# A decoder's second layer: the attention sink added by the tensor engine, the cosine product left in PSUM, and a small subtraction moved to GpSimd

## The reference, cut to what matters

```
x = x + _L1_attn_ref(layernorm(x), ...)          # "D" below
x = x + _L1_xattn_ref(layernorm(x), ctx, ctx, ...) # "E": attention of each row's 16 heads among themselves
x = x + _L1_ffn_ref(layernorm(x), ...)           # "F": causal attention that gates a two-branch product, then "M"
...
att = einsum('bhqd,bhkd->bhqk', q, k) * hd ** (-0.5) + sink      # D, hd = 16, one sink value per head
att = softmax(att);  out = einsum('bhqk,bhkd->bqhd', att, v)
...
mod = 0.1 * tanh(attn @ A)                                        # F
gate = silu(h @ W_in.T + mod * (h @ A) @ B);  up = h @ W_up.T     # M
out = residual + (gate * up) @ W_down.T
```

## Time and profile before

| what | value |
|---|---|
| time, median of 3 runs | 3060.1 us (3059.43 to 3067.85) |
| the profiled execution, its own time | 3064.77 us, of which the span 3063.0 us |
| busy share of the span | PE 90%, PEld 75%, DVE 84%, ACT 64%, POOL 69% |
| granted PE clock, mean over the span | 0.951 |
| largest groups of layer two | POOL L1802 380.4 us, POOL L1795 358.6 us, DVE L2324 151.7 us |

### The profile page before, as it was taken

The page is one execution under the profiler, slowest core; times in us unless marked ns, Lnnn a source line. Parts: engine busy times, 40 slices in busy tenths (PEclk is TensorE's granted clock), DMA queues, the critical chain, the costliest instruction groups (busy, mean ns, idle before and its releaser), DMA issues. The chain is left out here.

```text
span 3063.0 us, 68267 instructions
## 1 busy us (share of the span) xinstructions
PE 2760.3 (90%) x22128; PEld 2307.7 (75%) x22128; DVE 2565.5 (84%) x5547; ACT 1954.2 (64%) x4120; POOL 2126.1 (69%) x2651
## 2 busy tenths in 40 slices
PE   6999999999999999999788499558899999999978
PEld 3888888888888888888455399436777777777767
DVE  6888888888888888888499577488999999999973
ACT  5888778788787878878344155345656565565642
POOL 5897666666666666666378455288888888888870
PEclk9999999999999999999899699768999999999999
DMA  4564344444344444443444599300000000000000
GB/s 144 172 206 161 130 151 130 149 133 150 128 130 145 142 138 142 147 138 112 139 152 145 190 334 336 132 14 19 17 27 19 27 19 25 21 24 22 20 5 11
DMA packets 186021, 340.09 MB, mean 111 GB/s; under 512 B 40810, under 2 KB 104179, under 8 KB 179075
## 3 DMA queue, kind: packets, MB, share of 16 engines
q1 hardware_dynamic: 179586, 319.55, 31.8%
q0 software_dynamic: 6144, 16.79, 1.8%
HBM read 264.67 MB, written 63.18 MB: 107 GB/s over the span
## 5 line engine op out<-in xcount | busy, mean ns | idle before, releaser
L1802 POOL TENSOR_TENSOR l_prod<-l_sco,l_kv 128x256 f32<-128x256 f32 x512 | 380.4, 783 | 43.3 <-DVE l_sco L2316 43.3
L1795 POOL TENSOR_TENSOR l_prod<-l_q,l_kv 128x256 f32<-128x256 f32 x512 | 358.6, 742 | 57.8 <-DVE l_att L2324 57.8
L718 DVE SCALAR_TENSOR_TENSOR a_cq<-a_PQ,a_taps,a_cq 128x504 f32<-128x504 f32 (+2 forms) x384 | 281.8, 734 | 75.9 <-ACT a_cq L584 66.8
L718 DVE SCALAR_TENSOR_TENSOR a_ck<-a_PK,a_taps,a_ck 128x504 f32<-128x504 f32 (+2 forms) x384 | 280.7, 731 | 9.6 <-ACT a_ck L584 0.3
L342 POOL TENSOR_TENSOR a_tq<-a_cq,a_tq 128x512 f32<-128x512 f32 x128 | 166.0, 1297 | 130.8 <-ACT a_tq L590 130.4
L329 POOL TENSOR_TENSOR a_hrs<-a_hve,a_neghalf 128x8 f32<-128x8 f32 x128 | 209.7, 1638 | 25.2 <-DVE a_hve L735 25.2
L485 PE MATMUL a_Y<-a_wo,a_og_parts 128*128 128x256 f32 x1536 | 207.2, 285 | 4.5 <-POOL a_og_parts L336 4.5
L412 PEld LDWEIGHTS a_X<-a_wv,a_xb 128*128 128x128 f32 x1536 | 199.9, 188 | 12.1 <-issue 1.2
L412 PE MATMUL a_PQ<-a_x_hi,a_wqk 128*128 (+1 forms) x512 | 196.2, 424 | 12.6 <-issue 11.9
L342 POOL TENSOR_TENSOR a_tk<-a_ck,a_tk 128x512 f32<-128x512 f32 x128 | 163.7, 1279 | 62.6 <-ACT a_tk L590 62.6
L412 PE MATMUL a_X<-a_wv,a_xb 128*128 128x256 f32 x1536 | 204.1, 282 | 0.8 <-DMA a_xb<-a_x_lo 0.8
(11 more groups left out here) (400 smaller groups left out, 8488.7 us busy)
## 6 DMA issues: line engine op xcount, KB each, us to landing
a_wqk<-qk_parts SPq DMA_DIRECT2D x112, 512.0 KB, 3.3
m_wgu<-gate_up_parts SPq DMA_DIRECT2D x39, 1024.0 KB, 7.5
a_wv<-v_parts SPq DMA_DIRECT2D x56, 512.0 KB, 3.7
a_wg<-g_parts SPq DMA_DIRECT2D x112, 256.0 KB, 3.3
a_wo<-o_parts SPq DMA_DIRECT2D x112, 256.0 KB, 2.9
a_dr<-decays SPq DMA_DIRECT2D x256, 64.0 KB, 2.5
m_hs<-sorted_rows SPq DMA_DIRECT2D x39, 256.0 KB, 6.5
sorted_outs<-m_ys SPq DMA_DIRECT2D x39, 256.0 KB, 6.8
```

The costliest lines, as they stand in the source:

```text
L718: nc.vector.scalar_tensor_tensor(out=acc, in0=src, scalar=taps[p][:, tap + k:tap + k + 1], in1=acc, op0=ALU.mult, op1=ALU.add).then_inc(s_ ...
L1795: nc.gpsimd.tensor_tensor(out=prod[:, h], in0=qv[:, h:h + 1, :].to_broadcast([P, H, HD]), in1=kk, op=ALU.mult).then_inc(S("E_pqk"), 1)
L1802: nc.gpsimd.tensor_tensor(out=prod[:, h], in0=sco[:, h:h + 1, :].to_broadcast([P, HD, H]), in1=vv, op=ALU.mult).then_inc(S("E_pav"), 1)
```

## The change

**Sink.** Before, DVE computed a maximum over the scores, then two 16-element steps that carried sink and scale (L2266, L2269), then the arguments (L2274). Now a product of a 3-row constant (`inverse3`, filled with 1/SC) and the sink split in three bf16 rows (`sink3`) puts sink/SC into the score bank over all 512 columns of each half, in place of a product of two columns that only opened the bank; the score products add to it. DVE takes the maximum and subtracts it. The scale moves into ACT's exponential. In F the 16-element step (L2271) goes in the same way. The sink's rows are split and stored with the biases of stage two (`b_in`, `bias_rows` are longer for it).

**Rotary embedding.** The sine product is written first, and the cosine product then overwrites P0 in PSUM, so each of the two additions has one operand in PSUM and one in SBUF. The bank P0 counts as free after the additions.

**Low part of the gate input.** `ft_gm_lo` moves from DVE's list to the end of POOL's, behind `gather`, with waits on all of POOL's earlier work ahead of it and on its own result behind it.

**Gather.** The indirect DMAs read their row numbers from `slots`; the copy, the two ordering multiplications and their waits go.

```
-        nc.tensor.matmul(SS[:, half, 0:2], identb[:], identb[:, 0:2], start=True, stop=False, skip_group_check=True)
+        nc.tensor.matmul(SS[:, half, :], inverse3[:], sink3[:, half, :], start=True, stop=False, skip_group_check=True)
...
-        nc.scalar.activation(ex[k][:], ex[k][:], ACT.Exp).then_inc(S(k + "_exp"), 1)
+        nc.scalar.activation(ex[k][:], ex[k][:], ACT.Exp, scale=SC).then_inc(S(k + "_exp"), 1)
...
-                nc.vector.tensor_tensor(out=qr[:], in0=P0[:, 0:QKD].rearrange("p (h d) -> p h d", d=HD), in1=cos,
-                                        op=ALU.mult).then_inc(S("D_rt"), 1)
                 nc.vector.tensor_tensor(out=rt[:].rearrange("p h (f j) -> p h f j", f=2), in0=x[:, :, ::-1, :],
                                         in1=sin.rearrange("p h (f j) -> p h f j", f=2), op=ALU.mult).then_inc(S("D_rt"), 1)
+                dve.wait_ge(S("D_rt"), 2 * t + 1)
+                nc.vector.tensor_tensor(out=qr, in0=qr, in1=cos, op=ALU.mult).then_inc(S("D_rt"), 1)
...
-                    nc.vector.scalar_tensor_tensor(out=ex[k][:], in0=ss, scalar=SC, in1=hm[k][:, 2, :].unsqueeze(2).to_broadcast([P, H, SEQ]),
-                                                   op0=ALU.mult, op1=ALU.add).then_inc(S(k + "_arg"), 1)
+                    nc.vector.tensor_tensor(out=ex[k][:], in0=ss, in1=hm[k][:].unsqueeze(2).to_broadcast([P, H, SEQ]),
+                                            op=ALU.subtract).then_inc(S(k + "_arg"), 1)
...
+            def ft_gm_lo(t):
+                for done, per, ahead in (("E_pqk", H, 4), ("E_pav", H, 3), ("F_rs", 1, 2), ("E_rs", 1, 5), ("D_rs", 1, 7)):
+                    pool.wait_ge(S(done), per * cap(t + ahead))
+                pool.wait_ge(S("F_gm3"), 3 * t + 2)
+                part = gm3[t // 2 % 2][:, t % 2 * P:(t % 2 + 1) * P]
+                nc.gpsimd.tensor_tensor(out=part[64:64 + R, :], in0=gmT[:], in1=part[0:R, :].bitcast(F32), op=ALU.subtract).then_inc(S("F_gm3"), 1)
+                pool.wait_ge(S("F_gm3"), 3 * t + 3)
...
-                           ("G", gather)])
+                           ("G", gather), ("Ft", ft_gm_lo)])
```

More of the change, by code:

```diff
@@ L811, in recurrence_and_experts @@
         wd_high, wd_low = sb("wd_high", [P, E, DC, D], F32R), sb("wd_low", [P, E, DC, D], F32R)
-        b_in, b_rest = sb("b_in", [P, 8]), sb("b_rest", [P, 8])
-        b_piece = some(3, "b_piece", [P, 8], BF16)
+        b_in, b_rest = sb("b_in", [P, 16]), sb("b_rest", [P, 16])
+        b_piece = some(3, "b_piece", [P, 16], BF16)
         wkv, bkv, kvs = sb("wkv", [P, DC, 2 * D]), sb("bkv", [3, 2 * D], BF16), some(2, "kvs", [P, 2 * D])
@@ L1649, in layer_one @@
         dwqk, dwv, dwo = sb("dwqk", [P, DC, QKD]), sb("dwv", [P, DC, 64]), sb("dwo", [P, DC, D])
-        rope, sink = sb("rope", [P, 2, HD]), sb("sink", [P, H])
+        rope = sb("rope", [P, 2, HD])
+        sink3, inverse3 = sb("sink3", [3, 2, BLK], BF16), sb("inverse3", [3, P], BF16)
         ewq, ewo = sb("ewq", [P, DC, D]), sb("ewo", [P, DC, D])
@@ L1745, in _ @@
         def _(sp):
-            for tensor, name in ((dwqk, "dwqk"), (rope, "rope"), (sink, "sink"), (headmask, "headmask"), (dwv, "dwv"), (dwo, "dwo")):
+            for tensor, name in ((dwqk, "dwqk"), (rope, "rope"), (headmask, "headmask"), (dwv, "dwv"), (dwo, "dwo")):
                 sp.dma_start(tensor[:], a[name]).then_inc(S("d_in"), 16)
+            sp.dma_start(sink3[:].rearrange("q b n -> q (b n)"), bias_rows[:, 4 * D:4 * D + H * SEQ]).then_inc(S("d_in"), 16)
             for tensor, name in ((fwo, "fwo"), (fa, "fa")):
@@ L1805, in gather @@
             def gather(t):
-                wait_if(pool, S("G_ready"), 2 * t)
                 wait_if(pool, S("G_x"), 2 * t)
[L1808 to L1812, removed]
                 for k in range(2):
                     nc.gpsimd.indirect_dma_start(got[k][:], None, outs[:, :],
-                                                 bass.IndirectOffsetOnAxis(ap=of_tile[:, k:k + 1], axis=0)).then_inc(S(f"G_in{k}"), 16)
+                                                 bass.IndirectOffsetOnAxis(ap=slots[:, t, k:k + 1], axis=0)).then_inc(S(f"G_in{k}"), 16)
+            def ft_gm_lo(t):
[5 more added lines that the diff above has]
+                pool.wait_ge(S("F_gm3"), 3 * t + 3)
             pool.wait_ge(S("masked"), 4)
             iterate(pool, [("F", power("F", 2)), ("Et", products_av), ("Dn", power("D", 1)), ("En", power("E", 1)), ("E", products_qk),
-                           ("G", gather)])
+                           ("G", gather), ("Ft", ft_gm_lo)])
         @block.tensor
@@ L1867, in scores @@
                                                     qk[k][rows, c, s * SEQ:(s + 1) * SEQ], kx[k][rows, c, s],
-                                                    start=k == "D" and c == 0, stop=True, skip_group_check=True)
+                                                    start=False, stop=True, skip_group_check=True)
                 return last
@@ L2336, in ft_gm @@
                                                op1=ALU.mult).then_inc(S("F_gm"), 1)
-            def ft_gm_lo(t):
-                dve.wait_ge(S("F_gm3"), 3 * t + 2)
-                part = gm3[t // 2 % 2][:, t % 2 * P:(t % 2 + 1) * P]
-                nc.vector.tensor_tensor(out=part[64:64 + R, :], in0=gmT[:], in1=part[0:R, :].bitcast(F32), op=ALU.subtract).then_inc(S("F_gm3"), 1)
             def f_x2lo(t):
@@ L2394, in _ @@
                           ("En", statistics("E", "D_x", 1)), ("Et", et_values(2)), ("Et", et_values(1)), ("Ft", ft_gm),
[L2395 removed]
+                          ("Et", et_values(3)), ("D", arguments("D")), ("Md", m_x), ("Et", et_x), ("Et", split_low)])
 def decoder(nc, a, x_in, out):
@@ L2428, in decoder @@
         outs = nc.dram_tensor("sorted_outs", (EXPERT_TILES * 2 * P, D), F32, kind="Internal").ap()
-        bias_rows = nc.dram_tensor("bias_rows", (3, 4 * D), BF16, kind="Internal").ap()
+        bias_rows = nc.dram_tensor("bias_rows", (3, 4 * D + 16 * SEQ), BF16, kind="Internal").ap()
         gu_parts = nc.dram_tensor("gate_up_parts", (8, P, 4 * 2 * D), F32, kind="Internal").ap()
```

34 lines of the change are left out of this document (13 added, 21 removed).

## The result

The change made the kernel slower: 3140.6 us (median of 4 runs, 3139.27 to 3143.81) against 3063.6 us for the kernel before in the same comparison, a ratio of 1.0252 with the interval [1.0234, 1.0269]. That is + 77 us where the prediction had + 106. The profiled execution spans 3137.6 us against 3063.0. The side, the place and the pattern came out as forecast; the sizes of some terms did not.

The account below looks back on a forecast made before the run. VectorE was taken to set the pace, in a loop with TensorE and GpSimd. 12 × (6.1 + 2.5) = 103, plus 12, less 9, gave + 106 on 3064.8: 3171 profiled, 3165 us median, range 3112 to 3208.

Parts of the forecast that it names:

- + 106: Whole kernel: 103 us for 12 waits with gathers, 12 for two without, less 9 for rounds outside these pairs.
- The side, the place and the pattern: Slower (chance 0.86); TensorE waiting for GpSimd's low part at the head of its round; in every second round.
- The step that decides: Head of TensorE's list, every second round: it stands 8 to 9 us for the low part behind GpSimd's products and gather.
- long round: Third-stage round with TensorE's wait for the low part: 38.0 us instead of 30.97, before the clock's 2.5.
- X: The moment in a round when GpSimd's score products end; the long round's terms are counted from it.
- the clock's: Half block behind each wait, run at the 1.2 GHz level: + 2.5 us a pair, between 0 and 5.
- the pair's 61.94: Two third-stage rounds of the old kernel at 30.97 us each; a pair with the change was put at 68.0.
- The late waits: Rounds 31 and 33, waits without a gather ahead, 2.8 us shorter: 2 × (8.6 − 2.8) = 12 us.
- the rounds outside the pairs: Some nine rounds outside the pairs with a wait gain about 1 us each: − 9 us.
- The round without a wait: Every other third-stage round: TensorE's own work 29.9 us, VectorE about the same; taken as 30.0.
- Not felt: Rival: low part ready when TensorE is, so the kernel gains, TensorE bounding at 30.0 a round: 3031 us; chance 0.09.
- The clock holds: Rival: the wait is there but the clock does not fall: + 71, 3131 us; chance 0.15.

Follow-up runs that it names:

- experiment 1: The changed kernel with the gate input's low part back on VectorE, behind D's arguments: 3026.0 us, 0.9879 of the kernel before.
- experiment 2: The changed kernel with the low part still on GpSimd, but ahead of the score products: 3032.1 us, 0.9892 of the kernel before.
- 3: The changed kernel with the low part on GpSimd between the score products and the gather: 3120.6 us, 1.018 of the kernel before.
- 7: The changed kernel with M's first half block later in TensorE's list, behind D's values, and ScalarE's tanh moved too: 3091.5 us, 1.0085 of the kernel before.
- experiment 6: The changed kernel with 34 unread products on TensorE ahead of the wait for the low part, in 11 pairs: 3124.1 us, 1.0198 of the kernel before.
- experiment 8: The changed kernel with the low part on VectorE and the two-column product for the sink product, D's sink left out: 3020.0 us, 0.9856 of the kernel before.
- experiment 4: The kernel before with only the low part moved, to the end of GpSimd's list: 3211.7 us, 1.0481 of the kernel before.
- experiment 5: The changed kernel with 26 unread products on TensorE ahead of the wait for the low part, in 11 pairs: 3137.3 us, 1.0225 of the kernel before.

## Why the prediction was right, and by how much it was off

**The step that decides was right.** The wait is where it was put (TensorE at the head of its round, for GpSimd's low part), in every second round, 7.6 us where 8 to 9 was said, with D's values, VectorE's division, the weights of E and GpSimd's next products behind it. Experiments 1 and 2 show that it is the whole loss, 3 that its length scales the loss; 7 fits with the price being what is queued behind it. VectorE was spared as forecast: rotary products and additions take 2483.23 − 2481.51 = 1.72 (1.70 said), the additions 0.42 each, and the 16-element steps are gone. In a long round this turns into 8.24 of waiting at `l_recD`.

**The long round, term by term.** From X = 2455.92 + 10.94 = 2466.86:

| term | predicted | measured in after |
|---|---|---|
| X to TensorE's start | 3.5 | 2469.87 − 2466.86 = 3.01 |
| to D's values | 7.39 + clock 2.5 | 2478.23 − 2469.87 = 8.36 |
| hand-over | 0.1 | 0.11 |
| to E's weights | 1.85 | 2480.20 − 2478.34 = 1.86 |
| to the last sum | 12.70 | 2492.83 − 2480.20 = 12.63 |
| to the next products, and these | 1.37 + 11.07 | 1.37 + 11.05 |
| sum | 40.5 | 38.4 |

**The term that was mis-sized most is the clock's.** The prediction took 2.5 us from the one row of before in which a half block ran at half speed throughout. In after the granted clock was 0.50 only in the first 3.2 us of it, and the half block took 2474.43 − 2469.87 = 4.56 against 3.18 in the next round: 1.4 in this round, 1.6 on average by the twelve half blocks and by experiment 6; only in one of the twelve was the half block slow to its end. The lower end of the term, 0, was too low and 2.5 too high by 0.9 to 1.1. The rest of the difference is two small ones: the gather begins 0.14 behind the products, since the 0.46 of issue time before it, kept in the sum, went with the small steps; and from the half block to D's values 3.80 were enough, against 4.18 in the earlier trace rows. Together 2 us in each of 12 long rounds, 24 us.

**The round of before was too clean.** 30.97, on which the pair's 61.94 rests, is the most frequent round of before, but the 24 rounds average 31.27, because some took 31.6, most of them beside short spells at half clock. Against 62.54 a pair costs 0.6 less than against 61.94, 7 us over 12. With the 24 that is 31 of the 31.4 between the sum's + 106 and the spans' + 74.6 (profiled executions of both).

**Two misses that cancel.** The late waits were + 12 in the sum and the rounds outside the pairs − 9; measured are + 9.7 and, with start, first rounds and tail, − 7.3. That these nearly cancel is luck. Against the same rounds of experiment 1 the two late waits cost 6.8 (36.65 against 29.89) and 0.1: by the order of the lists no tile of D is left in round 33 whose values the weights of E would wait for, and the prediction charged that wait in full.

**What was exact.** The round without a wait was exact (30.0 said, 29.99 measured), and so was its reason, by experiment 8.

**The rivals.** "Not felt" needed the low part some 5 us before X; with it there (experiment 2), or on VectorE (1), the kernel takes 3026 to 3032, as that rival's 3031 said. "The clock holds" was 3131; experiment 6, which fills 11 of the waits, took 3124. Both are right as prices and wrong as forecasts. The sign rested on one count of what stands ahead of a 0.45 us instruction in its new list. The Trainium skill's advice to work on the engine with the highest occupancy first (Perfetto Trace Analysis, Identifying the Most-Contended Engine) names VectorE here. It was relieved of about 3.3 us a round (95.65% of 31.27 before, 77.5% of 34.28 after, over 2300 to 2900 us), and the kernel lost 77 us.

## What to carry to other kernels

Before a step is moved to an idler engine, count what stands ahead of it in that engine's list at the moment when its reader wants it; 13 us of products and gathers ahead of a 0.45 us subtraction cost more than all the rest gained. Price a wait by what is queued behind it and by who waits for that, down to where the loop closes, and take the clock's term from several rows, not from the worst. Work saved on the busiest engine counts only as far as no other engine fills the same piece of the loop: 0.96 us of the rotary embedding were worth 26 us, 1.64 us of steps behind the last sum, where GpSimd needs 4.1 of 4.9 us, only 17.

## What the runs showed of the chip that was not expected

After idles of 7.4 to 9.6 us the granted clock came back to 1.00 between 3.0 and 5.9 us behind the start of the half block in the twelve long rounds of after, so that this took 4.5 to 5.7 us; in experiment 4, after 8.6 to 9.7 us, it took 4.9 to 5.7. An idle of some 2 us behind dense filling made it fall in seven rounds of eleven (experiment 5); with some 0.4 us left (3.7 in 10) it held in all eleven. What decides between these is open; no run here tells it.

The low part took 0.45 us on GpSimd in most rounds, but 0.62 to 0.73 in 2 of 32 in after and in 11 of 32 in experiment 4. In each of these 13 VectorE had begun `l_sco<-l_sco,l_se` (128x256, both operands in SBUF) with it or up to 0.11 us before. Where that step began behind the low part, the low part took 0.45, and the step up to 0.72 instead of 0.42. On VectorE the same subtraction took 0.80 in 27 rounds of before, where one of GpSimd's products had begun ahead of it, and 0.28 in the five where none had. So in these rows it is the neighbour that started first that made such a step dear; no edit tried it.

The parts' gains do not add either. Alone, rotary, sink and gather shorten the round by 1.07, 0.55 and 0 us, which would make 29.35; together it is 29.95, where by experiment 8 TensorE bounds. In times that is 26, 17 and 5 us (the last within its uncertainty) against 40, no more apart than the uncertainties.
